# Attention scores per head on eight places of TensorE, transposed probabilities of half height in the same PSUM banks, and a new order of the TensorE queue

## The reference

```python
# L0 and L3, 12 heads of 32 features
q, k, v = (x @ Wq.T), (x @ Wk.T), (x @ Wv.T + bv)          # split into heads
scores = einsum('bqhd,bkhd->bhqk', q, k) * 384**-0.5 + bias # bias from adj
p = nan_to_num(softmax(where(any(scores != 0), scores, -inf)))
out = einsum('bhqk,bkhd->bqhd', p, v).reshape(b, n, 384) @ Wo.T + bo
# L1
scores = q @ k.T / sqrt(32) + beta * adj, masked to -9e15 where adj <= 0
out = softmax(scores) @ v
```

## Time and profile before

| | |
|---|---|
| median of 3 runs | 2837.92 us (2832.22 to 2837.97) |
| the profiled execution | 2831.32 us, of which the span of the trace is 2829.6 us |
| TensorE busy (matmuls) | 93% |
| VectorE busy | 77% |
| GpSimd busy | 68% |
| ScalarE busy | 51% |
| mean granted clock of TensorE | 0.976 of full speed |

### The profile page before, as it was taken

The page is one execution under the profiler, slowest core; times in us unless marked ns, Lnnn a source line. Parts: engine busy times, 40 slices in busy tenths (PEclk is TensorE's granted clock), DMA queues, the critical chain, the costliest instruction groups (busy, mean ns, idle before and its releaser), DMA issues. The chain is left out here.

```text
span 2829.6 us, 67112 instructions
## 1 busy us (share of the span) xinstructions
PE 2625.7 (93%) x22942; PEld 2333.2 (82%) x22942; DVE 2167.9 (77%) x3795; ACT 1445.6 (51%) x2968; POOL 1920.3 (68%) x2229
## 2 busy tenths in 40 slices
PE   7999999977999999689999979999898899999997
PEld 6888888866777777589999978888887688888886
DVE  4888888874888888757777757888888478888887
ACT  4555555535555555344444434445544455555553
POOL 2777777772666656657777748888887277777776
PEclk9999999998999999889999989999999999999999
DMA  3222222112222222131212122222321122222211
GB/s 106 72 69 68 70 68 68 60 48 86 83 74 76 74 73 75 56 99 57 68 55 66 56 97 75 82 78 77 91 77 56 56 69 72 68 70 68 68 60 49
DMA packets 179135, 200.54 MB, mean 71 GB/s; under 512 B 56517, under 2 KB 179017, under 8 KB 179017
## 3 DMA queue, kind: packets, MB, share of 16 engines
q1 hardware_dynamic: 179016, 198.99, 22.8%
HBM read 136.03 MB, written 62.91 MB: 70 GB/s over the span
## 5 line engine op out<-in xcount | busy, mean ns | idle before, releaser
L418 PE MATMUL l_ps_p<-l_xT,l_w 128*128 128x512 f32 x2592 | 678.7, 407 | 16.7 <-ACT l_qT L559 8.7
L1097 PE MATMUL l_ps_h<-l_w,l_hT 128*128 128x384 f32 x3456 | 676.1, 341 | 0.0
L1097 PEld LDWEIGHTS l_ps_h<-l_w,l_hT 128*128 128x128 f32 x3456 | 606.0, 189 | 2.0
L418 PEld LDWEIGHTS l_ps_p<-l_xT,l_w 128*128 128x128 f32 x2592 | 468.8, 189 | 124.0 <-ACT l_qT L559 16.0
L345 POOL TENSOR_TENSOR l_pr<-l_sc,l_st 128x768 f32<-128x768 f32 x192 | 283.0, 1474 | 390.4 <-DVE l_st L693 390.4
L315 POOL TENSOR_TENSOR v<-v,l_bvs 128x768 f32<-128x768 f32 x192 | 375.6, 1957 | 0.0
L1005 POOL TENSOR_TENSOR l_hp<-l_hf,l_hp 128x384 fp32r<-128x384 f32 x256 | 282.3, 1103 | 132.2 <-ACT l_hp L1189 128.6
L412 PE MATMUL l_ps_p<-l_w,l_xT 128*128 128x384 f32 x1728 | 341.5, 344 | 21.1 <-ACT l_k L565 17.6
L578 ACT ACTIVATE v<-l_ps_p 64x192 f32<-64x192 f32 x768 | 249.0, 324 | 175.5 <-PE l_ps_p L412 168.4
L700 DVE TENSOR_REDUCE l_st<-l_pr 128x12 f32<-128x768 f32 x192 | 182.8, 952 | 202.8 <-ACT l_pr L611 200.0
L1189 ACT ACTIVATE l_hp<-l_hf 128x384 fp32r<-128x384 f32 x256 | 134.5, 525 | 397.8 <-DVE l_hf L1314 397.5
(11 more groups left out here) (129 smaller groups left out, 4701.2 us busy)
## 6 DMA issues: line engine op xcount, KB each, us to landing
rows<-l_yo SPq DMA_DIRECT2D x256, 192.0 KB, 1.9
l_xa<-rows SPq DMA_DIRECT2D x64, 768.0 KB, 5.1
l_xr<-rows SPq DMA_DIRECT2D x192, 192.0 KB, 2.4
l_xa<-in_x SPq DMA_DIRECT2D x16, 768.0 KB, 5.1
l_xr<-in_x SPq DMA_DIRECT2D x64, 192.0 KB, 2.4
out<-l_yo SPq DMA_DIRECT2D x64, 192.0 KB, 1.9
l_edge<-in_adj SPq DMA_DIRECT2D x80, 128.0 KB, 2.3
raw<-in_L_gnn_Wq SPq DMA_DIRECT2D x3, 576.0 KB, 5.8
```

The source lines that it names most:

```text
L418: last = nc.tensor.matmul(bank[:, :], W[m][:, l, t, o * P:(o + 1) * P], rows[:, r, t, :], start=c + t == 0, stop=c == 2 and t == KT - 1)
L1097: last = nc.tensor.matmul(ps_h[m][:, :D], hT[gpar][:, l, t, s * P:(s + 1) * P], W[m][:, r, t, :], start=c + t == 0, stop=m != SELF and c = ...
```

## The change

Five things change in `attention_pass`, and the loads with them.

1. Each head's scores are made by a matmul of their own, 32 rows of contraction, 64 columns out and 64 columns through: 24 for each unit instead of 12 of 64 rows and 128 columns, with `tile_position` on four row places by two column places. `k2` and `even_odd` go; `kT` is written by one ScalarE instruction a step. The heads are renumbered (`head_of`), so that the three heads of one row place lie in one PSUM bank.
2. The probabilities are transposed by twelve transposes of 64 rows (one for each pair of heads and graph) instead of six of 128.
3. Scores and transposed probabilities of all heads share four banks, 170 columns a head. So the scores also wait until the copies of the transposed probabilities of n-2 are done (`act_pT`), and the transposes until the scores of n are evicted (`dve_sc`).
4. TensorE's order in a unit becomes: chunk 0, scores, values, chunk 1, transposes, chunk 2, output. `AHEAD` and `BETWEEN` change as shown; ScalarE's order follows, with the exponential behind the copies of the transposed probabilities. VectorE's and GpSimd's orders stay.
5. Wv and Wo are loaded in the order of the new head numbers: twelve transfers for each of them (rows for Wv and columns for Wo in L0 and L3, columns for Wv in L1), and the bias of v is loaded by twelve transfers in each pass instead of two.

Not shown below: the values read `pT` at 2t + r instead of 3r + t, the reciprocal of L1 (L715) and its scaled eviction (L729) take over the permutation of the heads, and VectorE's eviction reads the same 64 columns a head from four banks.

```diff
@@ -30,10 +30,18 @@
 ROWS = P * UNITS
 LN_EPS = 1e-5
 LN_EPS_INNER = 1e-12
-HEAD_STEP = 84
+HEAD_STEP = 170
 MASKED = -9000000000000000.0
 
 SPLIT = ((0, 0), (1, 0), (0, 1))
+
+
+NATURAL, ROWS_BY_SLOT, COLUMNS_BY_SLOT = range(3)
+
+
+def head_of(slot):
+
+    return 4 * (slot % KT) + slot // KT
 
 
 def counted(value):
...
@@ -116,11 +118,26 @@
 
     def load(self, sp, mats, free=None):
 
-        for m, mat in enumerate(mats):
+
+        for m, (mat, order) in enumerate(mats):
             if free:
                 free(m)
-            sp.dma_start(self.raw[m][:, :, :], mat.rearrange("(t p) n -> p t n", p=P)).then_inc(self.s_raw[m], 16)
-            self.loads[m] += 1
+            if order == ROWS_BY_SLOT:
+                for slot in range(HEADS):
+                    t, b = divmod(slot, 4)
+                    head = head_of(slot)
+                    sp.dma_start(self.raw[m][32 * b:32 * b + 32, t, :], mat[32 * head:32 * head + 32, :]).then_inc(self.s_raw[m], 16)
+                self.loads[m] += HEADS
+            elif order == COLUMNS_BY_SLOT:
+                for t in range(KT):
+                    for q in range(4):
+                        natural = mat[t * P:(t + 1) * P, :].rearrange("p (k m d) -> p m k d", m=4, k=KT)[:, q, :, :]
+                        sp.dma_start(self.raw[m][:, t, 96 * q:96 * q + 96].rearrange("p (k d) -> p k d", k=KT),
+                                     natural).then_inc(self.s_raw[m], 16)
+                self.loads[m] += 4 * KT
+            else:
+                sp.dma_start(self.raw[m][:, :, :], mat.rearrange("(t p) n -> p t n", p=P)).then_inc(self.s_raw[m], 16)
+                self.loads[m] += 1
 
 
...
@@ -176,10 +193,9 @@
         sbias = [a.sb(f"sbias{b}", [P, UNITS, NODES]) for b in range(2)]
 
         qT = [a.sb(f"qT{b}", [P, KT, ROWS]) for b in range(2)]
-        k2 = [a.sb(f"k2{b}", [P, KT, 2, ROWS]) for b in range(2)]
-        v2, even_odd = shared.v2, shared.even_odd
+        kT = [a.sb(f"kT{b}", [P, KT, ROWS]) for b in range(2)]
+        v2 = shared.v2
         qkb = a.sb("qkb", [P, 2, KT])
-        kbm = a.sb("kbm", [P, 2, KT])
 
         sc = [a.sb(f"sc{b}", [P, HEADS, NODES]) for b in range(2)]
         pr = [a.sb(f"pr{b}", [P, HEADS, NODES]) for b in range(2)]
@@ -193,9 +209,9 @@
         ln = [a.sb(f"ln{b}", [P, 10]) for b in range(2)]
         yo = [a.sb(f"yo{b}", [P, D]) for b in range(2)]
 
-        ps_s = a.ps("ps_s", [P, 2 * 512])
-        logits = ps_s[:, 8:8 + HEADS * HEAD_STEP].rearrange("p (h x) -> p h x", x=HEAD_STEP)
-        ps_t = a.ps("ps_t", [P, 2 * 512])
+        ps_s = a.ps("ps_s", [P, 4 * 512])
+        by_head = ps_s[:, 8:8 + HEADS * HEAD_STEP].rearrange("p (h x) -> p h x", x=HEAD_STEP)
+        logits, turned = by_head[:, :, :NODES], by_head[:, :, NODES:2 * NODES]
         ps_o = a.ps("ps_o", [P, 512])
         ps_y = a.ps("ps_y", [P, 512])
         ps_p = [a.ps(f"ps_p{b}", [P, 512]) for b in range(2)]
...
 
-        AHEAD = (("q", 0), ("x", 0), ("q", 1), ("q", 2), ("x", 1), ("k", 0), ("k", 1), ("k", 2), ("x", 2),
+        AHEAD = (("q", 0), ("q", 1), ("x", 0), ("q", 2), ("k", 0), ("x", 1), ("k", 1), ("k", 2), ("x", 2),
                  ("v", 0), ("v", 1), ("v", 2), ("v", 3))
-        BETWEEN = (((), (0,), (1, 2)), ((), (3,), (4, 5)), ((6,), (7,), (8, 9)), ((10,), (11,), (12,)))
+        BETWEEN = (((0,), (1,), (2,)), ((3,), (4,), (5,)), ((6,), (7,), (8, 9)), ((10,), (11,), (12,)))
 
         def exists(i, pos):
             return inside(i + (2 if AHEAD[pos][0] == "x" else 1), groups)
@@ -249,10 +266,11 @@
         def _(sp):
             sp.dma_start(xa[:, :, :], src_g[0]).then_inc(s_xa, 16)
             sp.wait_ge(c_zero, 1)
-            for odd in range(2):
-                heads = bv.rearrange("(a h o d) -> a h o d", a=1, o=2, d=32)[:, :, odd, :]
-                sp.dma_start(bvs[64 * odd:64 * odd + 64, :, 32 * odd:32 * odd + 32],
-                             heads.to_broadcast([64, PAIRS, 32])).then_inc(s_small, 16)
+            for slot in range(HEADS):
+                h, odd = divmod(slot, 2)
+                head = bv.rearrange("(a d) -> a d", a=1)[:, 32 * head_of(slot):32 * head_of(slot) + 32]
+                sp.dma_start(bvs[64 * odd:64 * odd + 64, h, 32 * odd:32 * odd + 32],
+                             head.to_broadcast([64, 32])).then_inc(s_small, 16)
             if bo is not None:
                 sp.dma_start(bos[:, :], bo.rearrange("(a d) -> a d", a=1).to_broadcast([P, D])).then_inc(s_small, 16)
             for j, b in enumerate(row_bias_cols or ()):
...
@@ -419,39 +437,37 @@
                                                     start=c + t == 0, stop=c == 2 and t == KT - 1)
                 last.then_inc(pe_p, 1)
 
-            def scores_may(n, i, s):
-
-
-
-                if not inside(n, units):
-                    return
+            def scores(n, i, par, s):
+
+
+
                 if s == 0:
                     pe.wait_ge(act_qk, 6 * (i + 1))
                 if counted(n):
                     pe.wait_ge(dve_sc, n)
-
-            def scores(n, par, s):
+                if counted(2 * (n - 1)):
+                    pe.wait_ge(act_pT, 2 * (n - 1))
                 for t in range(KT):
                     for g in range(GPU):
-                        for r in range(2):
-                            c, q = s * P + g * NODES, slice(64 * r, 64 * r + 64)
-                            h = PAIRS * r + 2 * t
-                            last = nc.tensor.matmul(logits[g * NODES:(g + 1) * NODES, h:h + 2, :NODES],
-                                                    qT[par][q, t, c:c + NODES], k2[par][q, t, :, c:c + NODES],
-                                                    start=True, stop=True)
+                        for m in range(4):
+                            c, q = s * P + g * NODES, slice(32 * m, 32 * m + 32)
+                            last = nc.tensor.matmul(logits[g * NODES:(g + 1) * NODES, KT * m + t, :],
+                                                    qT[par][q, t, c:c + NODES], kT[par][q, t, c:c + NODES],
+                                                    start=True, stop=True, tile_position=(32 * m, g * NODES))
                 last.then_inc(pe_s, 1)
 
             def probs_T(n, b):
                 if not inside(n, units):
                     return
                 pe.wait_ge(pool_p if wo else act_e, n + 1)
+                pe.wait_ge(dve_sc, n + (2 if inside(n + 1, units) else 1))
+                pe.sem_inc(pe_waited, 1)
                 for h in range(PAIRS):
-                    if h in (0, 4):
-                        if counted(2 * n - 1 + (h == 4)):
-                            pe.wait_ge(act_pT, 2 * n - 1 + (h == 4))
-                    last = nc.tensor.transpose(ps_t[:, h * P:(h + 1) * P], pr[b][:, 2 * h:2 * h + 2, :], ident[:, :])
-                    if h in (3, 5):
-                        last.then_inc(pe_t, 1)
+                    for g in range(GPU):
+                        q = slice(g * NODES, (g + 1) * NODES)
+                        last = nc.tensor.transpose(turned[:, PAIRS * g + h, :], pr[b][q, 2 * h:2 * h + 2, :], ident[q, q])
+                        if h == PAIRS - 1:
+                            last.then_inc(pe_t, 1)
 
             def values(n, par, s):
                 if not inside(n, units):
...
@@ -508,19 +524,14 @@
                 for s in range(UNITS):
                     n = i * UNITS + s
                     ppar, ps = (par, s - 2) if s >= 2 else (1 - par, s + 2)
-                    scores(n, par, s)
+                    fill(i, par, s, 0)
+                    scores(n, i, par, s)
                     values(n - 2, ppar, ps)
-                    fill(i, par, s, 0)
+                    fill(i, par, s, 1)
                     probs_T(n - 1, 1 - s % 2)
-                    fill(i, par, s, 1)
-                    if s < UNITS - 1:
-                        scores_may(n + 1, i, s + 1)
-                    else:
-                        scores_may(n + 1, i + 1, 0)
+                    fill(i, par, s, 2)
                     output(n - 2, ps % 2)
-                    fill(i, par, s, 2)
-
-            scores_may(0, 0, 0)
+
             over_groups(pe, groups, group)
             values(units - 2, 1, UNITS - 2)
             probs_T(units - 1, 1)
...
@@ -560,13 +570,10 @@
                         else:
                             i = nc.scalar.activation(qT[gpar][:, o, :], bank[:, :], ACT.Copy)
                     else:
-                        for j in range(2):
-                            if row_bias_cols:
-                                i = nc.scalar.activation(k2[gpar][:, o, j, :], bank[:, :], ACT.Identity,
-                                                         bias=kbm[:, j, o:o + 1], scale=even_odd[:, j:j + 1])
-                            else:
-                                i = nc.scalar.activation(k2[gpar][:, o, j, :], bank[:, :], ACT.Copy,
-                                                         scale=even_odd[:, j:j + 1])
```

(36 more changed lines are left out.)

29 lines of the change are left out of this document (11 added, 18 removed).

## The result

The changed kernel takes 2947.98 us (median of 4 runs, 2942.44 to 2951.55), the kernel before beside it 2835.33: ratio 1.0396, 95% interval 1.0373 to 1.0419. It is slower, as forecast, and slower than forecast: 2912 stood in the prediction, 2848 to 3010 was its range. The profiled execution took 2942.44 us, its span is 2940.7 us; before it was 2829.6. So 111 us of span are to be found.

A forecast was written before the change was run, and what follows sets the result against it. TensorE's order was taken as the bound in L0, VectorE next. L0 and L3 +30, L1 +44 and starts +7 gave +81 us on 2831.3: 2912 us, own range 2860 to 2950, wider range 2848 to 3010.

The forecast's parts named there:

- Part 5: Waits said to cost nothing: transposes on the scores' eviction, covered by a projection (up to 1 us a unit uncovered); single k copy.
- Part 3: New TensorE order: v1 waits for VectorE's subtraction of x2, 1.2 us in L0, 3.8 in L1; +1.07 and +1.44 us a group.
- Part 4: In L1, v1 and unit 3's scores run at 1.2 GHz after the wait: +1.7 us a group, bounds 0 to 3.
- The rival in which the clock holds: L1 keeps its clock despite the wait: 2888 us, inside the likeliest range; no chance of its own.
- Parts 1 and 2: TensorE in each unit: 48 score loads in 0.35 us, twelve transposes in 0.50, with idle 0.37 us ahead and 0.17 behind.
- over 0.6 us: Sign that the prediction is wrong: the 48 score loads take longer than this, where 0.35 us was taken.
- The rival in which small matmuls don't overlap: Scores take 1.28 us, +0.93 in each of 192 units: 3050 us, or 3150 to 3200 with slow transposes; chance 0.14.
- Part 6: Starts of L0 and L1: more weight and bias loads, 5 us later each, single k copies give back 3; +7 us.
- VectorE in time: x2's subtraction ends before v1 wants its bank, so waits and clock loss go: about 2800 us, chance 0.12.
- the change gives back what it costs: Free drains and transposes of 0.33 us, -0.7 us a unit, partly swallowed by the wait: about 2840 us, chance 0.07.

The follow-up runs named there:

- moving v1 alone: Changed kernel with v1 put behind the scores of unit 3 instead of ahead of them: 2881.64 us, ratio 1.0159 to the kernel before.
- the edges alone: Changed kernel with VectorE's work on the next group's edges moved from unit 2 to unit 3: 2903.3 us, ratio 1.025 to the kernel before.
- both together: Changed kernel with v1 behind the scores of unit 3 and the next group's edges in VectorE's unit 3: 2846.71 us, ratio 1.004 to the kernel before.

## Why the prediction was right, and where it was too small

The medians of the four combinations, us:

| | order before | order changed |
|---|---|---|
| parts before, loop | 2835 | 2923.7 |
| parts before, straight | 2824.9 | 2898.4 |
| parts changed, loop | 2906.7 | 2948.0 |
| parts changed, straight | 2835.8 | 2876.3 |

"Parts" are the small matmuls, transposes, banks, copies and loads. Without jumps the order costs 73 us on the old parts and 41 on the new. The new parts cost 11 us with the old order, where the traces have the two starts 12 us later and the passes together 1 us shorter, and give back 22 with the new one. With the loop, the new parts cost 72 and 24. The loop costs 10 us before, 25 with the order alone, and 71 or 72 with the new parts. The 25 stand in L1, without a stall at a jump and with 71 packets on q8: a loop costs time also where its body is held, there because v1 waits longer and the clock falls more often behind it.

The last column is the same difference between the two kernels without loops.

| term, us | forecast | measured in the traces | without loops |
|---|---|---|---|
| L0 and L3 | +30 | +41 | +1.5 |
| L1 | +44 | +51 | +34 |
| starts | +7 | +16 | +18 |
| L2 and end | 0 | +3.5 | +0.7 |
| sum | +81 | +111 | +54 |

**The sum lacked a term: the jump of the loop.** Part 5 lists what costs nothing and says nothing of the length of the instruction stream; that is the step that failed. Straight code takes 26.0, 16.5 and 18.1 us off the three passes. About 0.6 us in each of the 28 groups of L0 and L3 is the earlier VectorE; the other 44 us are the 15 jumps at about 3 us, slow clock behind them included (47 us by the long groups).

**Luck had a share in the number.** The forecast's 81 us name only things that are there without the jumps too, and without them its terms come to 54: L0 and L3 to almost nothing where +30 stood, L1 to 10 less than forecast, the starts to 11 more. The terms that were too large made up in part for the one that was missing; with the jumps added to them as they stood the forecast would have been some 2960. In L0 and L3 a plain group is 0.6 us longer with the loop and 0.2 without, not 1.07; the first group of a pass is 1.3 us shorter, and the next to last, put at nothing, 1.9 us shorter, in L1 even 5.0.

**Part 3, the wait of v1: right in place and releaser.** L1: 3.8 forecast, 3.90 measured; wanted 6.6 us behind the scores (6.44), released 10.5 us behind them (9.8 to 10.7). A plain group there is 35.5 us, forecast 35.9. In L0 the size was off: 0.72 us, not 1.2, and plain groups of 37.5, not 38.0. v1 is wanted 0.19 us later than taken and VectorE is 0.3 sooner. That moving v1 alone and the edges alone shorten this wait, that both together leave 0.2 us of it, and that in L1 the order alone makes it, shows it; the wait is 52 of L1's 557 us.

**Part 4, the clock: right.** +1.4 us a group in L1 (1.7 taken), none in the plain groups of L0 and L3. The rival in which the clock holds is out: the granted clock of the group in L1 is 0.95, and that of the earlier trace rows was 1.00. How long the idle time was did not settle alone what became of the pace: behind the 3.9 us v1 took over 3 us in most groups, but behind 2.38 us, or 2.62 in the order alone without loop, it now did and now kept its 1.84.

**Parts 1 and 2: sizes off in both directions.** 48 score loads take 0.64 us, as long as the 24 of before, not 0.35. The prediction had named "over 0.6 us" as a sign that it is wrong, and so it was in this term: half the columns on twice the places took as long. What a unit gains here is 0.11 us, the pause ahead of the values that went. Twelve transposes take 0.45 us, and the 0.17 us behind them doesn't come. The rival in which small matmuls don't overlap (1.28 us) is out. The Trainium skill's "TensorE: Matmul & The Clock Gate" (Wait — 56ns, not 53.3ns?) has a floor of about 25 ns from start to start; here 48 loads in 0.64 us are 13 ns apart, so that for these quarter-height tiles the measurement decides against the rule. The Trainium skill's "TensorEngine Tiling (Array Packing)" (Tiling Modes, Key Properties) has the engine drain when the mode changes; the trace agrees where the tiles get smaller, with 0.36 us ahead of the half-height transposes, which the 128-row ones didn't have, and shows no such pause where they get larger again, ahead of the values and behind the transposes.

**Part 5's wait of the transposes on the eviction** is covered by the projection, as said. Without that cover (the old order on the changed parts) the transposes stand 0.31 us in straight code, which the change of tiles alone would explain, and with the loop 0.25 to 0.5 us now and then.

**Part 6, the starts: less than half of what was measured.** 24 ordered loads cost SyncE 13.6 us and twelve bias loads 7.5; 0.47 to 0.66 us each, as taken, but the block opened at 16.16 instead of 8.68, near the far end of the 3 to 9 us. The projection that now stands ahead of the first scores, 2.3 us, was left out, and of the 3 us given back by single k copies the traces show 0.8 at the start of L1 (v waits 0.34 us for a k copy there, 1.10 before).

The rivals "VectorE in time" and "the change gives back what it costs" are out with the waits and pauses above. What stays open: why a jump now costs 1.3 us and now 4.6 in the same loop, why some of it shows as ScalarE's copy of v being late (1.34 us at 276.08), at what length between some 710 and 880 matmuls a loop stops being held, and where the rest of the microsecond a group goes that the order alone costs in L0.

## What to carry to other kernels

When a queue is reordered, walk the release of every buffer in it against the other engine's queue, which was not reordered; the wait sits where the next user of a bank has come closer, and what stands behind it in the queue (here the scores) carries it to a third engine. Count the instructions of a loop's body before and after a change that splits work into smaller pieces, and look at the packets of the instruction queue: if they grow with the number of turns, write the loop out or shorten the body. Test parts and order crosswise: in the loop the parts alone cost 72 us and the order alone 89, and yet with one projection and the edges moved, the loop written out and the loads spread, the same parts made the kernel 1.3% faster (1.0% against the kernel before without its loop).

## What the runs showed of the hardware

- A loop of two groups of L0 is some 710 TensorE matmuls before and 950 after, each with a weight load (two groups of the earlier trace rows and of the window above). By the packets on q8 the first is held (71, straight code 186) and the second fetched in every turn (230, straight code 231), and each jump costs about 3 us. In L1 the held body is some 640 and the one that stalls 880. With four groups of the old size, some 1,420 matmuls, it is 193 packets and 6 us a jump. That the packets are this fetching, and that it is what the jump waits for, is inferred from their number and from where the stalls stand.
- Straight code that is fetched all the way, 3.78 MB of it, shows no stall in the steady groups of L0 and L3.
- The clock falls behind idle time by issue as behind a wait for another engine: after 2.81 us of it nine matmuls of 128x512 took 3.87 us instead of 2.33.
- Waits of one length can end either way. Of 13 waits of 2.6 us in L1, in one execution of the order alone without loop, v1 kept its pace of 1.85 us behind eight, took 2.1 to 2.3 us behind three and 3.2 behind two; behind waits of 2.6 to 3.1 us with the loop it took over 3 us 11 times of 13.
- In the loop VectorE's eviction started 1.30 us behind the scores, in straight code 0.82. Which part of the loop makes up the 0.48 us was not tried.
